# Ternary weight signs: from a stage of their own into the heads loop of the first attention layer

## The reference

```python
def _L0_ffn_ref(x, W_up, W_gate, W_down):
    def ternary_quant(w):
        scale = jnp.mean(jnp.abs(w)) + EPS
        q = jnp.clip(jnp.round(w / scale), -1.0, 1.0) * scale
        return w + jax.lax.stop_gradient(q - w)
    wu = ternary_quant(W_up)
    wg = ternary_quant(W_gate)
    wd = ternary_quant(W_down)
    up = jnp.einsum('bsd,ed->bse', x, wu)
    gate = jnp.einsum('bsd,ed->bse', x, wg)
    hidden = jax.nn.silu(up) * gate
    return jnp.einsum('bse,de->bsd', hidden, wd)
```

## Time and profile before

| | |
|---|---|
| median of 3 runs | 1602.89 us (1595.99, 1602.89, 1606.72) |
| the profiled execution's own time | 1595.93 us |
| its span | 1594.2 us |
| busy, share of the span | TensorE 86%, VectorE 59%, ScalarE 42%, GpSimd 16% |
| heads loop of the first attention, first to last exponential | 58.0 to 231 us |
| output projection and norm | 233.3 to 248.8 us |
| making of the signs | 250.0 to 268.9 us |
| feed-forward f0, first instruction | 269.2 us |

### The profile page before, as it was taken

One profiled execution on the slowest core, in us unless ns is written; L12 is line 12 of the kernel. 1 busy time (PEld: TensorE's weight loads), 2 busy tenths in 40 slices (PEclk: granted clock), 3 DMA queues, 4 the chain that ended last, 5 costly groups with the idle time before them and its releaser, 6 DMA issues. The chain is left out here.

```text
span 1594.2 us, 31153 instructions
## 1 busy us (share of the span) xinstructions
PE 1364.8 (86%) x12875; PEld 757.9 (48%) x12883; DVE 939.4 (59%) x2146; ACT 672.7 (42%) x952; POOL 258.5 (16%) x342
## 2 busy tenths in 40 slices
PE   7999993987360995898999989999689999989999
PEld 3355551463240874464455545436235555564435
DVE  3999957744787225664999944432445555525331
ACT  4577772634340111553777762110434444442110
POOL 4300000000208003004200000110333433200110
PEclk9999996998555597999999998999779999999999
DMA  3122111000312100002222030000300000000000
GB/s 90 31 39 42 23 45 67 1 12 0 99 38 50 29 4 1 14 1 57 35 39 40 15 95 0 0 8 0 60 9 15 14 17 13 9 2 1 0 0 27
DMA packets 51647, 41.54 MB, mean 26 GB/s; under 512 B 26465, under 2 KB 41810, under 8 KB 51506
## 3 DMA queue, kind: packets, MB, share of 16 engines
q1 hardware_dynamic: 51506, 39.55, 11.5%
HBM read 20.23 MB, written 3.43 MB: 15 GB/s over the span
## 5 line engine op out<-in xcount | busy, mean ns | idle before, releaser
L560 DVE TENSOR_REDUCE row_max_pieces<-psum 128x1 f32<-128x512 f32 (+3 forms) x672 | 406.6, 647 | 120.1 <-PE psum L455 117.8
L657 ACT ACTIVATE probs<-psum 128x1024 f32<-128x1024 f32 (+7 forms) x384 | 343.5, 899 | 220.7 <-PE psum L455 220.7
L509 PE MATMUL psum<-probs,v_ones 128*32 128x256 f32 (+1 forms) x2688 | 238.9, 376 | 6.4 <-POOL probs L444 4.1
L455 PE MATMUL psum<-q_all,k_head 97*32 97x512 f32 (+3 forms) x1536 | 192.3, 492 | 3.5 <-issue 3.5
L455 PE MATMUL psum<-k_stack,q_stack 96*32 96x512 bf16 x2048 | 162.5, 387 | 5.3 <-DVE row_max_pieces L560 2.9
L455 PE MATMUL psum<-q_stack,k_stack 97*32 97x512 bf16 x2048 | 160.5, 385 | 0.0
L509 PEld LDWEIGHTS psum<-probs,v_ones 128*32 128x32 f32 x2688 | 88.5, 109 | 81.8 <-POOL probs L444 21.1
L455 PE MATMUL psum<-k_head_bf,q_all_bf 80*32 80x512 bf16 (+3 forms) x768 | 95.6, 344 | 4.7 <-POOL q_all_bf L2267 2.8
L455 PEld LDWEIGHTS psum<-q_all,k_head 97*32 97x32 f32 x1536 | 78.8, 110 | 34.1 <-issue 8.4
L455 PEld LDWEIGHTS psum<-k_stack,q_stack 96*32 96x32 bf16 x2048 | 57.7, 97 | 72.5 <-DVE row_max_pieces L560 20.4
L1865 PE MATMUL psum<-lora_in,arena 128*128 128x512 f32 (+1 forms) x192 | 87.9, 596 | 3.4 <-DVE lora_in L1944 3.4
(11 more groups left out here) (317 smaller groups left out, 2058.7 us busy)
## 6 DMA issues: line engine op xcount, KB each, us to landing
q_stack<-arena SPq DMA_DIRECT2D x32, 96.0 KB, 2.7
k_stack<-arena SPq DMA_DIRECT2D x32, 96.0 KB, 2.7
arena<-gd_g_sums SPq DMA_DIRECT2D x6, 512.0 KB, 5.9
q_stack<-arena SPq DMA_DIRECT2D x32, 64.0 KB, 2.3
k_stack<-arena SPq DMA_DIRECT2D x32, 64.0 KB, 2.3
x_tokens<-in_x SPq DMA_DIRECT2D x4, 256.0 KB, 4.0
k_stack<-arena SPq DMA_DIRECT2D x32, 32.0 KB, 2.3
q_stack<-arena SPq DMA_DIRECT2D x32, 32.0 KB, 2.0
```

Source lines behind the costliest of these rows:

```text
L455: last = pe.matmul(o[j:j + 32], by[:, j:j + 32], rows, **flags)
L509: last = pe.matmul(psum[32 * g:32 * g + VW, PVB, a - g * D:D], V[:, c, h, :], pr[:, n % PB, a:(g + 1) * D], start=(c == 0), stop=(c == (2 ...
L560: last = dve.reduce_max(mx[:, h % 2, qt, i:i + 1], o[:, 0:plain], AX.X)
L657: act.activation(pr[:, n % PB, q_from(c):], psum[:, 2 * (n % 2):2 * (n % 2) + 2, :].rearrange("p a n -> p (a n)")[:, q_from(c):], ACT.Exp, ...
```

## The change

A class `Ternary` replaces both functions. Its buffers for the signs are there from the start, and raw weight, magnitudes and sides lie in buffers of the heads block, apart from the arena. Each weight is cut into four slices of 128x512.

- SP (`load`): ahead of the row of head 1, 6 and 11 and behind the stack copies of the turn before, it issues one raw weight (1024 KB). The second and the third first wait until GpSimd has made all signs of the weight before, since there is one raw buffer.
- ScalarE (`act`): behind the exponential of c = 1 and c = 5 of heads 1, 2, 6, 7, 11 and 12 it takes the magnitudes of one slice and accumulates their sum; 12 instructions.
- GpSimd (`pool`): behind its preparation, per weight, it adds the four sums over the partitions (`partition_all_reduce`), makes the scale in five small steps that each wait for the one before, and then per slice the low side, the high side and their difference; 12 instructions of 128x512.
- `project_out` of the first attention issues no transfers, and the block `ternary_weights` is gone.

```diff
-def ternary_raw(core, wup_d, wgate_d, wdown_d):
...
-def ternary_weights(nc, core, scope, w, loaded):
...
+    HEADS_EACH, FROM = HEADS // 3, 1
...
+    def load(self, sp, h):
+        i = h // self.HEADS_EACH
+        if h % self.HEADS_EACH == self.FROM and i < 3:
+            if i:
+                sp.wait_ge(self.signed, SLICES * i)
...
+    def act(self, act, n):
+
+        h, c = n // NT, n % NT
+        i, j = h // self.HEADS_EACH, 2 * (h % self.HEADS_EACH - self.FROM) + c // 4
+        if i < 3 and c % 4 == 1 and 0 <= j < SLICES:
+            if j == 0:
+                act.wait_ge(self.loaded[i], 16)
+            if i + j:
+                act.wait_ge(self.summed, SLICES * i + j)
+            act.activation(self.magnitudes[:], self.raw[:, j, :], ACT.Abs,
+                           accum_out=self.sums[:, j:j + 1]).then_inc(self.summed, 1)
+
+    def pool(self, pool):
...
+        for i, signs in enumerate((self.ups, self.gates, self.downs)):
+            pool.wait_ge(self.summed, SLICES * (i + 1))
+            t, scale = self.totals, self.scale[:, i:i + 1]
+            link(pool.partition_all_reduce(t[:], self.sums[:], P, bass.bass_isa.ReduceOp.add))
...
+            for j in range(SLICES):
+                n = SLICES * i + j
+                if n >= 2:
+                    pool.wait_ge(self.signed, n - 1)
+                pool.tensor_scalar(self.side[:, j % 2, :], self.raw[:, j, :], self.half[:, 1:2], None,
+                                   ALU.is_lt).then_inc(self.low, 1)
+                pool.tensor_scalar(self.high[:, j % 2, :], self.raw[:, j, :], self.half[:, 0:1], None,
+                                   ALU.is_gt).then_inc(self.low, 1)
+                pool.wait_ge(self.low, 2 * n + 2)
+                pool.tensor_tensor(flat[:, j, :], self.high[:, j % 2, :], self.side[:, j % 2, :],
+                                   ALU.subtract).then_inc(self.signed, 1)
...
                 for h in range(HEADS):
+                    if aside:
+                        aside.load(sp, h)
                     sp.wait_ge(ring_out, turn_place(h) + 1)
```

More of the change, by code:

```diff
@@ new lines, with __init__, begin, link @@
+SLICES = 4
+class Ternary:
+    HEADS_EACH, FROM = HEADS // 3, 1
+    def __init__(self, core, sources, scope):
+        self.core, self.sources = core, sources
+        self.scale = core.sb("ternary_scales", [P, 3], F32, scope)
+        self.ups = core.sb("w_up_signs", [P, KT, DE], BF16, scope)
+        self.gates = core.sb("w_gate_signs", [P, KT, DE], BF16, scope)
+        self.downs = core.sb("w_down_signs", [P, NE, D], BF16, scope)
+    def begin(self, scope):
+        core, n = self.core, KT * DE // SLICES
+        self.raw = core.sb("ternary_raw", [P, SLICES, n], F32, scope)
+        self.side, self.high = core.sb("low_side", [P, 2, n], BF16, scope), core.sb("high_side", [P, 2, n], BF16, scope)
+        self.magnitudes = core.sb("magnitudes", [P, n], BF16, scope)
+        self.sums = core.sb("abs_sums", [P, SLICES], F32, scope)
+        self.totals = core.sb("abs_totals", [P, SLICES], F32, scope)
+        self.half = core.sb("half_scales", [P, 2], F32, scope)
+        self.loaded = [core.sem(f"ternary_w{i}_loaded") for i in range(3)]
+        self.summed, self.total, self.low, self.signed = (
+            core.sem("ternary_" + n) for n in ("abs_summed", "total", "low_side", "signs"))
+    def load(self, sp, h):
[3 more added lines that the diff above has]
+                sp.wait_ge(self.signed, SLICES * i)
+            d, k = self.sources[i], (KT, KT, NE)[i]
+            sp.dma_start(self.raw[:].rearrange("p s n -> p (s n)").rearrange("p (k n) -> p k n", k=k),
+                         d.rearrange("(k p) n -> p k n", p=P)).then_inc(self.loaded[i], 16)
+    def act(self, act, n):
[9 more added lines that the diff above has]
+    def pool(self, pool):
+        steps = [0]
+        def link(instruction):
+            steps[0] += 1
+            instruction.then_inc(self.total, 1)
+            pool.wait_ge(self.total, steps[0])
+        for i, signs in enumerate((self.ups, self.gates, self.downs)):
+            pool.wait_ge(self.summed, SLICES * (i + 1))
+            t, scale = self.totals, self.scale[:, i:i + 1]
+            link(pool.partition_all_reduce(t[:], self.sums[:], P, bass.bass_isa.ReduceOp.add))
+            link(pool.tensor_tensor(t[:, 0:2], t[:, 0:2], t[:, 2:4], ALU.add))
+            link(pool.tensor_tensor(t[:, 0:1], t[:, 0:1], t[:, 1:2], ALU.add))
+            link(pool.tensor_scalar(scale, t[:, 0:1], 1.0 / (DE * D), TERNARY_EPS, ALU.mult, ALU.add))
+            link(pool.tensor_scalar(self.half[:, 0:1], scale, 0.5, None, ALU.mult))
+            link(pool.tensor_scalar(self.half[:, 1:2], scale, -0.5, None, ALU.mult))
+            flat = signs[:].rearrange("p k n -> p (k n)").rearrange("p (s n) -> p s n", s=SLICES)
+            for j in range(SLICES):
[9 more added lines that the diff above has]
+                                   ALU.subtract).then_inc(self.signed, 1)
@@ L259, in ternary_ffn @@
 def ternary_ffn(nc, core, tag, weights, loads):
-    scale, ups, gates, downs = weights
+    scale, ups, gates, downs = weights.scale, weights.ups, weights.gates, weights.downs
     X, XNT, psum = core.X, core.XNT, core.psum
@@ L383, in attention_heads @@
 def attention_heads(nc, core, tag, causal, V, O, q_max, k_max, keys, queries, shift_row, exp_kw,
-                    shift_dt, mask=None, head_loads=None, prep=None, rope=None):
+                    shift_dt, mask=None, head_loads=None, prep=None, rope=None, aside=None):
     psum, ident = core.psum, core.ident
@@ L429, in attention_heads @@
             masked = sem("probs_masked")
+        if aside:
+            aside.begin(tmp)
         ring_in, ring_out = sem("ring_filled"), sem("ring_taken")
@@ L438, in _ @@
                     prep.pool(pool)
+                    if aside:
+                        aside.pool(pool)
                     if causal:
@@ L659, in _ @@
                                    ACT.Exp, **exp_kw).then_inc(e_done, 1)
+                    if aside:
+                        aside.act(act, n)
                 keep_out(HEADS - 1)
@@ L681, in attention16_early, with attention16 @@
     return wq, wk, loaded, loads
-def attention16(nc, core, tag, early, wv_d, wo_d, biases, gates, pos_d, next_loads):
+def attention16(nc, core, tag, early, wv_d, wo_d, biases, gates, pos_d, next_loads, aside=None):
     X, XNT, psum, ident = core.X, core.XNT, core.psum, core.ident
@@ L2359, in build @@
         load_inputs(nc, core, a["x"], first[-1])
-        raw, raw_loaded, raw_loads = ternary_raw(core, a["f_up"], a["f_gate"], a["f_down"])
+        ternary_scope = ExitStack()
+        ternary = Ternary(core, (a["f_up"], a["f_gate"], a["f_down"]), ternary_scope)
         attention16(nc, core, "aa", first, a["a_wv"], a["a_wo"], {"bqk": a["a_bqk"], "bv": a["a_bv"], "bo": a["a_bo"]},
-                    {"justice": a["a_justice"], "order": a["a_order"]}, a["pos"], raw_loads)
+                    {"justice": a["a_justice"], "order": a["a_order"]}, a["pos"], None, ternary)
         core.layer_done()
-        ternary_scope = ExitStack()
-        ternary = ternary_weights(nc, core, ternary_scope, raw, raw_loaded)
         delta = gated_delta_early(core, "gd", of("g_"))
```

2 lines of the change are left out of this document (1 added, 1 removed).

## The result

The changed kernel takes 1585.66 us (median of 4 runs, 1578.86 to 1586.81), the kernel before 1603.43 us (4 runs). The ratio is 0.9897 with a 95% interval from 0.987 to 0.9924: faster by 1.0%, as forecast (1583 us, 1575 to 1593). Beside the experiments both ran again: 1585.45 (6 runs) against 1600.93 (12 runs), ratio 0.9892 (0.9863 to 0.992).

The account below looks back on a forecast made before the run. The block ahead of f0 was wholly on the path; in the heads loop TensorE and VectorE were full, GpSimd free. Removing it gives -19.2 us, ScalarE's new work +2.6: -16.6 from 1599.4, so 1583 us, range 1575 to 1593.

Parts of the forecast that it names:

- The removed block: Ahead of feed-forward f0: without the block of signs, f0 starts at 250.03 in place of 269.23, 19.2 us earlier.
- the seam of f1: Ahead of feed-forward f1, the norm's end to f1's start takes 1.25 us without a block; taken as f0's future gap.
- The loop, 2.6 us: Heads loop: six magnitudes ahead of the finished head's copy stall TensorE 0.60 us each, net 0.44, in all 2.6 us.
- the wait of 0.16 us ahead of the transpose: Three groups after the stall, transpose L477 waited 0.16 us for VectorE; this was to absorb part of each stall.
- The 0.60 us of one magnitude: ScalarE in the heads loop: one queued 128x512 magnitude instruction adds about 0.60 us, by the busy time of L318.
- The six behind c = 5, nothing: Heads loop: six magnitudes delay the next exponential 0.3 us each, but key scores have 0.9 us of cover; cost nothing.
- GpSimd, 12 to 23 us per weight: GpSimd's differences, compares, small steps and all-reduce per weight take 14 us, range 12 to 23, hidden beside the heads loop.
- the sentence on the Trainium skill: GpSimd library switches around each all-reduce might add 6 to 12 us per weight: 26 from the middle, 35 at the end.
- The margin that I had worked out: GpSimd's work per weight delays nothing up to 24 us, only the weight up to 30; the last weight has 32.
- the first rival: Heads loop pays more, through GpSimd and VectorE contention or slow accumulation: loses 7.5 us, gain 11.7, time 1588; 17 in 100.
- The rival of a late GpSimd: GpSimd work T per weight above 31 us delays rows of heads 6 and 11, then the loop's end; 5 in 100.
- The sum: Whole kernel: -19.2 + 2.6 = -16.6 us from a middle of 1599.4, giving 1582.8, rounded 1583.

Follow-up runs that it names:

- experiment 7: Changed kernel with only the magnitudes behind c = 1 moved behind c = 2, those behind c = 5 left: loop 166.49 us, time 1582.34 us (1 run, another chip).
- experiment 4: Changed kernel with GpSimd making both compares of every slice twice: 1615.21 us, ratio 1.0079 to the kernel before.

## Why the prediction was right, and where not

- **The removed block, 19.2 us: right.** 19.33 from the profiled pair. Taking the seam of f1 for that of f0 was the step that made this exact (1.25 forecast, 1.07 to 1.13 seen in all profiles with the change).
- **The loop, 2.6 us: right mechanism, size off.** It measured 3.17 to 3.23, six times 0.53 to 0.54. The step that failed is the wait of 0.16 us ahead of the transpose, which I had read as a wait for VectorE and counted as absorbed: with the stall it came back as 0.14 us (131.72 against 131.58), and in the changed kernel VectorE is no longer named for it ([0.42 <-issue]). What it is stays open. A smaller error went the other way and cancelled a part: the stall was 0.54 and not 0.60. In the kernel before the weight load stood 0.09 us ahead of a matmul that waited for its turn, and now 0.03 us ahead of one that didn't, so there was a cover of 0.06 us where I had seen none. (The load's own row gives 0.21 as its idle time; behind the copy's end it came after 0.12, and the matmul after 0.21, which is what my sum used.)
- **The 0.60 us of one magnitude: right by two errors that cancel.** Queued, the activation takes 0.52 us to the next start, and the read of the accumulator, an instruction of 0.19 us that no row of mine had, adds 0.10.
- **The six behind c = 5, nothing: right**, by experiment 7.
- **GpSimd, 12 to 23 us per weight: wrong, without a consequence.** It took 26.4. A compare was priced at 0.8 us, at most 1.19 by scaling one of 128 columns, and took 1.57; that is 6.2 us over eight. The hole behind the all-reduce, 7.1 us, was only in the sentence on the Trainium skill. That sentence's 26 us meets the 26.4 by luck: it had two holes of 6 us and cheap compares, and the trace has one hole of 7.1 and dear ones. The margin that I had worked out (30 us, some 32 at the end) was what kept the forecast right: SP waited 2.6 and 1.6 us for GpSimd, and no row of a head was late. Against the forecast the second weight was still on its way when the row behind it was issued (118.21 + 5.0 = 123.2 against 122.06), but no key scores waited for it. VectorE's maxima (L586) beside GpSimd's work kept their median of 0.681 us, so the contention of the first rival didn't come.
- **The rival of a late GpSimd** didn't happen, but experiment 4 shows that it is real. Its price was mis-sized: 2 (T - 31) + (T - 32) with T = 39 gives 23, and 29.8 came by the medians, 24.9 + 7.2 = 32.1 by the trace. The term of the rows was 24.9 in place of 16: it left out the time from a late row's issue to its use and TensorE's slow clock after the wait.
- **The sum.** -16.6 forecast; the medians give -17.8 and -15.5 in the two comparisons. The seam and the loop by the traces, 19.33 - 3.2 = 16.1, are closer to it than either; the difference to the medians is within their intervals. The number itself was 2.7 us low: the middle that I started from (three runs and the profiled one, 1599.4) lay 4.0 below the median of four (1603.43), and the larger gain in the medians took 1.2 of that back. That the two partly cancel is luck.

## What to carry to other kernels

Work given to an engine with a quarter of its time free cost nothing or nearly all of its length here (0.54 of 0.62 us), by its place. Look at which of its instructions another engine starts on within one or two tenths of a microsecond, and put nothing ahead of those. A chain on a slow, idle engine needs its margin worked out from both ends, and then checked by making the chain longer; past the margin the price was higher than the delay alone, as TensorE came out of the wait at half its clock. Two single profiles don't give a gain of 1%: here they showed 9 us of 16, for the time of another stage varied by 6. Compare the stages that the change touches.

## What the runs showed that I had not expected

- A compare of 128x512 with a scale per partition takes GpSimd 1.57 us, whether it writes bf16 or f32, and is slower than the difference of two tensors of that size (1.16 us with bf16 inputs, 1.28 with f32).
- After a partition all-reduce GpSimd's next ordinary instruction comes after 6.8 to 7.8 us of idle time, at each of 21 switches in seven profiles, and a second all-reduce ahead of the switch costs 0.54 us only.
- An activation with an accumulator is followed by one of 0.19 us that reads it, of which 0.10 lengthens the queue.
- With the first weight's transfer in flight the row of head 1 was issued at 65.49 to 65.98 us in seven profiles, without it at 65.00 to 65.26 in three. Some 0.5 us seem to go there; the cause wasn't tested.
